# A fused attention and expert kernel: eight expert tiles on a table from five of eight groups' counts, the last w2 pieces in finished buffers, loads in another order

## The reference

```python
x = x + attn(_layernorm(x))   # below, per token t, 4 heads, dk 128, dv 64
    pred = einsum('bhk,bhkv->bhv', k_t, S); delta = (v_t - pred) * beta_t
    S = S + k_t[..., :, None] * delta[..., None, :]; o_t = einsum('bhk,bhkv->bhv', q_t, S)
x = x + ffn(_layernorm(x))    # experts e = 0..7, hidden size 1024
    probs = softmax(x @ router.T); topk_vals, topk_idx = top_k(probs, 2)
    h = gelu(x_flat @ w1[eid].T); y = h @ w2[eid].T
    out = out + w[:, None] * y    # w is the token's gate for eid, or 0
```

## Time and profile before

| | us |
|---|---|
| median of three executions | 976.61 |
| lowest, highest | 975.64, 978.22 |
| the profiled execution | 973.25 |
| its span, first to last instruction | 971.4 |
| TensorE busy in the span | 855.0 (88%) |
| VectorE, ScalarE, POOL busy | 628.9, 601.8, 425.5 |

### The profile page before, as it was taken

The page is one execution under the profiler, slowest core; times in us unless marked ns, Lnnn a source line. Parts: engine busy times, 40 slices in busy tenths (PEclk is TensorE's granted clock), DMA queues, the critical chain, the costliest instruction groups (busy, mean ns, idle before and its releaser), DMA issues. The chain is left out here.

```text
span 971.4 us, 29866 instructions
## 1 busy us (share of the span) xinstructions
PE 855.0 (88%) x9998; PEld 671.8 (69%) x9999; DVE 628.9 (65%) x1822; ACT 601.8 (62%) x1636; POOL 425.5 (44%) x426
## 2 busy tenths in 40 slices
PE   0589999999999999999971699999999999998983
PEld 0368887788878877788751577777777777766762
DVE  3468888898989989898846354555555554534341
ACT  4578888898888888877642454455445544534430
POOL 3445555667767766754536023232323232222122
PEclk9999999999999999999965699999999999999997
DMA  5212222233233323211106123233232323222212
GB/s 196 66 50 87 64 73 89 79 100 100 84 96 99 106 82 92 88 46 46 46 34 220 56 39 48 47 53 51 44 49 44 59 44 50 45 46 41 39 18 28
DMA packets 49736, 66.58 MB, mean 69 GB/s; under 512 B 6416, under 2 KB 34192, under 8 KB 49616
## 3 DMA queue, kind: packets, MB, share of 16 engines
q1 hardware_dynamic: 35616, 46.33, 16.3%
q0 software_dynamic: 13424, 18.10, 10.7%
q10 hardware_dynamic: 576, 0.53, 0.2%
HBM read 41.46 MB, written 23.48 MB: 67 GB/s over the span
## 5 line engine op out<-in xcount | busy, mean ns | idle before, releaser
L646 POOL DMA_INDIRECT out<-wvg_s,yidx x71 | 113.7, 1601 | 317.7 <-DVE wvg_s L1911 169.0
L934 PE MATMUL ps<-w_s,wqk 128*128 128x128 f16 (+1 forms) x1336 | 240.0, 288 | 11.7 <-ACT wqk L663 9.0
L934 PE MATMUL ps<-x_s,w_hi 128*128 128x256 f16 (+1 forms) x1376 | 201.2, 256 | 0.1
L934 PE MATMUL ps<-x_s,w_lo 128*128 128x256 f16 (+1 forms) x688 | 170.2, 255 | 0.0
L1884 DVE SCALAR_TENSOR_TENSOR KpAT<-KQ,wqk 128x512 f16<-128x512 f32 (+1 forms) x144 | 98.7, 686 | 100.5 <-ACT wqk L663 100.4
L663 ACT ACTIVATE w_s<-ps 128x512 f16<-128x512 f32 (+2 forms) x288 | 147.8, 532 | 25.6 <-PE ps L934 10.4
L934 PE MATMUL ps<-w_s,KpAT 128*128 x568 | 155.7, 274 | 0.0
L934 PEld LDWEIGHTS ps<-w_s,wqk 128*128 128x128 f16 x1336 | 101.7, 98 | 77.9 <-issue 14.7
L934 PEld LDWEIGHTS ps<-x_s,w_hi 128*128 x1376 | 120.4, 98 | 18.4 <-issue 0.8
L663 ACT ACTIVATE x_s<-ps 128x512 f16<-128x512 f32 x36 | 21.5, 596 | 163.6 <-PE ps L1310 163.6
L910 ACT ACTIVATE KQ<-ps 128x512 f32<-128x512 f32 (+1 forms) x144 | 85.1, 591 | 48.1 <-PE ps L934 42.3
(11 more groups left out here) (185 smaller groups left out, 1792.0 us busy)
## 6 DMA issues: line engine op xcount, KB each, us to landing
wst<-w SPq DMA_DIRECT2D x56, 256.0 KB, 2.8
w_s<-eye SPq DMA_DIRECT2D x32, 256.0 KB, 2.7
rowA<-routed_rows SPq DMA_DIRECT2D x28, 260.0 KB, 2.7
x_s<-x SPq DMA_DIRECT2D x32, 128.0 KB, 2.6
out<-x_s SPq DMA_DIRECT2D x32, 128.0 KB, 1.7
rowA<-routed_rows SPq DMA_DIRECT2D x15, 130.0 KB, 2.1
KQ<-w SPq DMA_DIRECT2D x6, 256.0 KB
out<-wvg_s,yidx POOLq DMA_INDIRECT x71, 3.9
```

The lines of the kernel that those rows point to most:

```text
L646: pool.indirect_dma_start(out=out, out_offset=bass.IndirectOffsetOnAxis(ap=yidx[:, q, a:a + 1], axis=0), in_=yrow[:, q % 2, a, :], in_offs ...
L934: return pe.matmul(dst, lhsT, rhs, start=start, stop=stop, **kw)
```

## The change

**Start.** Each constant has a semaphore of its own, and SP issues x tile 0, the constants `fc`, wb and wq, x tile 1, and then the rest in the order of use; ScalarE's queue issues wk and wvg. The identities of Y come by three loads instead of ScalarE's fill, the masks arrive as int8, and the norm weight is tiled on the host. Layer norm and transposed input of tile 0 stand ahead of the weights' high halves. The weight pieces start four passes later.

The core of the diff:

```diff
+        late = sb("inverse_levels", [P, 2 * LATE * 2 * D], fp16)
+        w2_late = [wqk[...], kq_wvg[:, 2 * 4 * H * P:]...]       # w2's blocks m = 6 and 7
+        late_in = [wst[:, :], at_slot(0), at_slot(1), wvg_flat[:, 0:PIECE], wvg_flat[:, PIECE:2 * PIECE], at_slot(2), at_slot(5), wst[:, :]]
 sync:
-                piece(2 * (i - 2) + 1)
-                piece(2 * (i - 1) + 0)
+                piece(2 * (i - 6) + 1)
+                piece(2 * (i - 5) + 0)
+            done(sp, s_kTp, T - 1)
+            late_piece(1)
...
+            sp.wait_ge(s_tab, 1)
+            load_rows(0, 0)
+            store(T - 3)
+            done(sp, s_rps, T - 1)
+            load_rows(0, 1)
...
+            sp.wait_ge(s_tail, 1)
-            for e in range(4):
+            for e in range(E):
                 pad(sp, e)
...
+            expert_body(0, 1)
+            sp.wait_ge(s_tab, 2)
             sp.wait_ge(s_pads, 16 * PADS)
 gpsimd:
+            late_lo(4)
+            o_rsqrt(T - 1)
+            scatter(T - 8, 0)
...
-                    value = i * 128 + (32 * q + 16 * a)
+                    value = i * 128 + (32 * q + (16 * a if split(i, q) else 0))
 scalar:
+                evac(late_entries(k)[:, :, 0, :], late_in[k].rearrange("p (m n) -> p m n", n=D), W_SCALE)
+                evac(late_in[k], late_in[k], W_SCALE).then_inc(s_whi, 1)
...
+            late_hi(4)
+            late_hi(5)
+
+            w_evac(T - 1)
+            ln2(T - 2)
             xT_hi(0, 0)
+            o_square(T - 1)
+            xn2T_evac(T - 2)
+            logits_copy(T - 2)
+            late_hi(6)
+            oT_evac(T - 1)
+            hidden(0, 0, range(0, 1))
+            late_hi(7)
             xT_hi(0, 1)
+            ln2(T - 1)
+            hidden(0, 0, range(1, 2))
+            xn2T_evac(T - 1)
+            hidden(0, 0, range(2, 3))
+            logits_copy(T - 1)
+            route_exp(T - 1)
+            hidden(0, 0, range(3, 4))
 tensor:
+                        w = w2_s[:, bass.ds(e + m * E, 1), :, :] if m < KH - 2 else w2_late[m - (KH - 2)][:, bass.ds(e, 1), :, :]
...
             xT_make(0, 0)
+            out_chunk(T - 1)
+            xn2T_make(T - 2)
+            pe.wait_ge(s_tab, 1)
+            up(0, 0, range(0, 2))
+            logits_make(T - 2)
+            up(0, 0, range(2, 4))
+            oT_make(T - 1)
+            up(0, 0, range(4, 6))
+            wo_make(T - 1)
             xT_make(0, 1)
+            up(0, 0, range(6, 8))
+            xn2T_make(T - 1)
+            logits_make(T - 1)
+            xT_make(0, 2)
+            up(0, 1)
+            rank(T - 1, p_rank_last, p_tot_last)
+            pe.wait_ge(s_whi, 2 * T)
+            down(0, 0)
 vector:
+            xT_lo(0, 2)
+            hidden_lo(0, 1)
+            positions(T - 1)
+            chosen_positions(T - 1)
+            slot_sums(T - 1)
+            slots(T - 1)
+            other_counts()
+            other_units()
+            other_table()
...
+            rows_out(0, 0)
```

More of the change, by code:

```diff
@@ L193, in build @@
[L193 to L198, removed]
+        tab = sb("tile_table", [P, 2 * ENTRIES], i32)
@@ new lines, in _, with load_rows @@
+            late_piece(0)
+            next_inverse(T - 1)
+            done(sp, s_kTp, T - 1)
+            late_piece(1)
+            late_piece(2)
+            store(T - 4)
+            done(sp, s_vgps, T - 1)
+            late_piece(3)
+            late_piece(4)
+            sp.wait_ge(s_ups, state_updates(T - 1))
+            late_piece(5)
+            done(sp, s_ops, T - 3)
+            late_piece(6)
+            sp.wait_ge(s_wlo, EARLY + 1)
+            late_piece(7)
+            def load_rows(i, q):
+                if split(i, q):
+                    for a in range(halves(i, q)):
+                        at = 2 * entry(i, q, a) + 1
+                        row = sp.value_load(tab[0:1, at:at + 1], min_val=0, max_val=SPARE)
+                        sp.dma_start(xg[q % 4][:, a, :], routed[bass.ds(row, P), :]).then_inc(s_xg[q % 4], 16)
+                    return
+                row = sp.value_load(tab[0:1, bass.ds(i * 8 + (2 * q + 1), 1)], min_val=0, max_val=SPARE)
+                sp.dma_start(xg[q % 4], routed[bass.ds(row, PE_TOK), :].rearrange("(a p) n -> p a n", p=P))\
+                    .then_inc(s_xg[q % 4], 16)
@@ L632, in _ @@
                 l_low(i - 2)
-            pool.wait_ge(s_pads, 16 * PADS)
+            ln2_scale(T - 4)
+            late_lo(0)
+            scatter(T - 11, 1)
+            o_rsqrt(T - 3)
+            scatter(T - 10, 0)
+            l_low(T - 1)
+            ln2_scale(T - 3)
+            late_lo(1)
+            scatter(T - 10, 1)
+            o_rsqrt(T - 2)
+            late_lo(2)
+            scatter(T - 9, 0)
+            ln2_scale(T - 2)
+            late_lo(3)
+            scatter(T - 9, 1)
+            late_lo(4)
+            o_rsqrt(T - 1)
+            scatter(T - 8, 0)
+            late_lo(5)
+            scatter(T - 8, 1)
+            late_lo(6)
+            ln2_scale(T - 1)
+            scatter(T - 7, 0)
+            late_lo(7)
+            scatter(T - 7, 1)
+            for m in range(T - 6, T):
+                for k in range(2):
+                    scatter(m, k)
             for c in range(XR):
@@ L898, in xT_hi, with hidden @@
                 evac(xTh[:, q % 2, :, :], p_gT).then_inc(s_gTh, 1)
-            def hidden(i, q):
-                for m in range(4):
+            def hidden(i, q, ms=range(4)):
+                for m in ms:
                     act.wait_ge(s_hps, i * 16 + (4 * q + m + 1))
@@ L1774, in _ @@
+            for i in range(T + 3):
+                if i == T - 1:
+                    dve.wait_ge(s_pos, FIRST_GROUPS)
+                    step(dve.tensor_copy(run_first[:, :], run[:, :]))
                 without_first(i - 8)
@@ L1918, in _ @@
[L1918 to L1921 removed]
+            o_scale(T - 1)
+            o_norm(T - 1)
+            oT_low(T - 1)
+            attention_residual(T - 1)
+            ln2_stats(T - 1)
+            dve.wait_ge(s_wlo, EARLY + 6)
+            hidden_lo(0, 0, range(0, 1))
+            xT_lo(0, 1)
+            hidden_lo(0, 0, range(1, 3))
+            best_logit(T - 1)
+            differences(T - 1)
+            best_marked(T - 1)
+            best_rank(T - 1)
@@ L1922, in expert_body @@
+            chosen_positions(T - 1)
[4 more added lines that the diff above has]
+            other_table()
+            def expert_body(i, first=0):
+                for q in range(first, 4):
                     if not (isinstance(i, int) and i * 4 + q + 2 >= TILES):
```

655 lines of the change are left out of this document (431 added, 224 removed).

## The result

| | before | after |
|---|---|---|
| median of five executions, us | 977.02 (975.64 to 978.22) | 937.14 (934.66 to 941.82) |
| profiled execution, span | 973.25, 971.4 | 941.82, 940.0 |
| TensorE busy in the span | 855.0 (88%) | 860.5 (92%) |

The ratio is 0.9592, with a 95% interval of 0.9565 to 0.9619. Measured again on another chip it was 0.9608 (0.9586 to 0.9630). The forecast of 936.7 was met within a microsecond, but not all of its terms were. The profiled execution of the new kernel was the slowest of its five.

A forecast was written before the change was run, and what follows sets the result against it. Only the start, the seam between attention and experts, and the last tiles could give time without less arithmetic. Start -16.5, last passes +2, seam -25.4 sum to -39.9: 976.61 to 936.7 us, own range 931 to 942, wider 926 to 949.

The forecast's parts named there:

- E: End of the last product of the attention's last pass on TensorE: 504.54 before, forecast near 490.
- The start: Kernel start up to the loop: first projection at 11.3 instead of 28.35; term -16.5 us, bounds -14 and -19.
- I charge 0.5: Start: 0.5 us for VectorE's three weight halves and copies before the loop's first operation.
- rival 2: Start given back: identities, masks and x rows come late, passes 1 to 3 stretch; start -9, 944.2 us; chance 0.06.
- Moving them four passes later is free there: Attention loop: weight pieces don't set the period, 14.28 us with them and 14.42 after; no cost.
- The last three passes: End of attention: first table on VectorE and late pieces on ScalarE mostly fall beside waits; +2 us, bounds 0 and 5.
- The seam: Between attention and experts: tile 0 runs in the tail's waits; 44.9 us from E instead of 70.3, term -25.4.
- rival 3: More gain than taken: head 18.5, no cost in the last passes, seam -29; 929.1 us; chance 0.12.
- ScalarE's part between 15.4 and 24.5: Seam, up to the last group's exponentials: 9.1 us of added ScalarE work, beside waits or in series; taken 19.5.
- Rival 1: Seam's chain in series, TensorE's wait lowers the clock: seam -18.5, last passes +5; 946.6 us; chance 0.20.
- Rival 4: Expert tiles: second product reads blocks 6 and 7 from another buffer, 1.31 us wait per tile; 983.9 us; chance 0.04.
- Rival 5: Seam: SP stands at a wait ahead of tile 0's rows, some 12 us lost; 948.7 us; chance 0.02.

The follow-up runs named there:

- c4_pieces_early: Changed kernel with the expert weight pieces starting four passes earlier again, as before the change; 950.72 us, ratio 0.9753 to the kernel before.
- b3_both: Changed kernel with tile 0's output ahead of the rest of the second table and tile 4's rows loaded before the pads; 935.79 us against 939.68.
- c1_delay: Changed kernel with sixteen idle POOL power operations ahead of the first layer norm; 954.72 us against 939.68.
- c3_weights_later: Changed kernel with wvg's and wo's halves made behind the squares of k of tile 0 instead of ahead; ratio 0.9550 to the kernel before.
- b1_rows_first: Changed kernel with only tile 0's output moved ahead of the rest of the second table; 941.08 us against 939.68.

## Why the prediction was right, step by step

The median was met, the way to it was not: E was forecast near 490 and came at 501.1 and 499.7, and a later E is what the prediction itself names as a sign of being wrong.

**The start: right at its milestone, incomplete behind it.** First projection forecast at 11.3, measured 11.72. The step that failed is "I charge 0.5" for what stands ahead of the loop's first operations. Weight halves and half clock cost 5.5, so the term of -16.5 measures -11.2, outside its own bounds of -14 and -19. By size this is nearer to rival 2 (-9), but not by its mechanism: identities and masks were never waited for, and TensorE's idle gap of 4.09 us was.

**The pieces.** "Moving them four passes later is free there" held less well than it read. Out 0 to out 29 took 413.5 and 414.6 us before, 413.7 with the pieces early, 419.2 and 417.1 in the changed kernel. Most passes are 14.1 to 14.5 us as forecast; the loss sits in single passes, in which ScalarE waits for a piece or the clock falls. All eleven traces with the changed kernel's pieces have 414.3 to 419.2, with a mean of 416.4, against 413.5 to 414.6 in the three with early pieces. So a loss of 2 to 3 us is likely and its mechanism is seen (a piece that lands late in certain passes), but with one trace of c4_pieces_early it isn't shown. And what the sentence left out is larger: without the pieces' going from the first four passes the start's gain is gone.

**The last three passes:** forecast +2, measured +1.6 and +2.2 against the mean of before. That fits in size, but the term isn't pure: in two traces of related kernels with the same table and late pieces (b3_both, c1_delay) it is 18.9, as before, where the low clock begins later (1.00 from 470 to 486 in b3_both, 0.50 from 482 to 486 in the changed kernel).

**The seam: right in mechanism, 3 us better than forecast,** nearly rival 3's -29. Its chain was ScalarE, then VectorE's second table, then tile 0's output, and the wait stood where it was forecast, released by the operation that was named.

| from E, us | forecast | measured |
|---|---|---|
| last group's Exp ends | 19.5 | 17.5 |
| last low half of tile 1 | 28.3 | 25.8 |
| second table | 35.9 | 33.3 |
| output of tile 0 | 38.7 | 35.7 |
| tile 1's second product ends | 43.9 | 41.2 |
| with tile 4's wait | 44.9 | 41.5 |

The term that was mis-sized is the first, ScalarE's part between 15.4 and 24.5: all but some 2 of its 9.1 us fell into waits. From there on each step is within 0.4 us, but for the last, 0.4 instead of 1.0. TensorE's wait was 3.03 instead of 4 (1.78 in the second trace), the rows of tile 4 came 0.36 late. The seam's worst bound is added up wrongly (44.9 + 5.0 + 2.7 + 1.5 is 54.1, not 53.1); nothing here hangs on it.

**Rival 1, the low clock in the seam,** did not come: TensorE's first blocks of tile 0 ran at half clock only until about 504 (0.50 from 500 to 504, 0.95 from 504 to 510). **Rival 4** is out: the earlier trace rows and the rows above have the same 10.88 us, and a split tile waits 1.30 as in the earlier trace rows. **Rival 5** too: the transposes of tile 0's rows start at 500.88, where the last pass ends.

So the right sum came in part by luck, of errors that cancel. Start (5.3 us) and middle (4.1) gave less, the seam 3.3 more, and the traced executions lie on opposite sides of their medians, by 5 us in sum (means of two). I had moved both kernels by the same 3.4 from execution to median, which a single traced execution does not justify.

## What to carry to other kernels

A milestone that moves is worth only what the next milestone moves: for a start, read the second iteration's operations and put the edit's halves apart, since sorted loads alone gave nothing behind the first projection and with the weight pieces back in their old place some 15 us of the gain were gone. When a wait is taken away, look for the one right behind it on another queue and take both, as the pair gave 3.9 us where one alone gave none. A gain of one traced execution is known no better than the executions spread, here some 7 us; the pieces between milestones, from two traces, are better evidence than the sum.

## What the runs showed of the hardware

- The granted clock does not follow the length of a gap alone. A wait of 4.09 us at 22 us was followed by half clock in every trace that has it unfilled; one of 2.50 in the kernel before by none in one trace (window 36 to 46 at 1.00) and by a fall in the other (0.70); one of 2.94 in c3_weights_later and one of 2.15 in b1_rows_first by falls; one of 3.21 in c1_delay by a fall too (0.73 from 549 to 552); one of 3.03 in the changed kernel by none (1.00 from 530 to 554).
- It also fell in the loop, where TensorE was busy 13.1 of 14.4 us in the pass before. What decides it there stays open.
- One power operation of POOL on 128x1 took 0.58 us at 6.50 and 1.55 at 12.40, beside VectorE's half of wq; on 128x8 it took 1.66 with and without this change.
